# One kernel of a vision tower: thirteen in place of ten gate-up products on GpSimd, and the last two maxima taken apart

## The reference

```python
def _act_fake_quant(x, clip_factor):
    scale = jax.nn.sigmoid(clip_factor) * jnp.max(jnp.abs(x)) / QMAX
    return jnp.clip(_ste_round(x / scale), -QMAX - 1.0, QMAX) * scale
...
xq = _act_fake_quant(x, clip_x[0])
gate = jnp.einsum('bsh,ih->bsi', xq, _weight_fake_quant(w_gate))
up = jnp.einsum('bsh,ih->bsi', xq, _weight_fake_quant(w_up))
h = _act_fake_quant(jax.nn.silu(gate) * up, clip_down[0])
return jnp.einsum('bsi,hi->bsh', h, _weight_fake_quant(w_down))
```

## Time and profile before

| | us |
|---|---|
| median of 3 runs | 151.08 (150.08 to 154.04) |
| the profiled execution | 151.07 |
| its span | 149.1 |
| busy in the span: PE, DVE, ACT, POOL | 119.8, 124.0, 81.4, 36.3 |
| gate-up stage, first matmul to the maximum over the columns | 98.8 to 125.8 |

### The profile page before, as it was taken

One profiled execution on the slowest core, in us unless ns is written; L12 is line 12 of the kernel. 1 busy time (PEld: TensorE's weight loads), 2 busy tenths in 40 slices (PEclk: granted clock), 3 DMA queues, 4 the chain that ended last, 5 costly groups with the idle time before them and its releaser, 6 DMA issues.

```text
span 149.1 us, 1974 instructions
## 1 busy us (share of the span) xinstructions
PE 119.8 (80%) x668; PEld 77.5 (52%) x668; DVE 124.0 (83%) x249; ACT 81.4 (55%) x153; POOL 36.3 (24%) x60
## 2 busy tenths in 40 slices
PE   0759979984978936999999987669999998798710
PEld 0749958972443614854587564235545333564400
DVE  0799998989899849923999798877989898999991
ACT  4004116231694677229961399966999980894000
POOL 6668991000000000000000000003556660005710
PEclk9999999996599998799999999987999999999975
DMA  3999500000000000000000000000000000001276
GB/s 97 388 421 420 228 4 2 0 0 0 0 0 0 7 0 0 0 0 0 0 0 4 0 0 0 0 0 4 0 4 0 0 0 0 4 0 70 85 226 181
DMA packets 2897, 8.01 MB, mean 54 GB/s; under 512 B 453, under 2 KB 709, under 8 KB 2760
## 3 DMA queue, kind: packets, MB, share of 16 engines
q1 hardware_dynamic: 2600, 7.37, 13.5%
q10 hardware_dynamic: 288, 0.52, 0.9%
HBM read 5.79 MB, written 2.10 MB: 53 GB/s over the span
## 4 chain that ended last, share of the span: by engine, by line
PE 35%; DVE 29%; ACT 22%; issue 7%; DMA 3%; POOL 1%; DVEq 0%; ACTq 0%; POOLq 0%
PE bank L557 8%; ACT early L787 7%; PE bank L473 6%; PE bank L413 5%; PE bank L541 4%; DVE middle L1226 4%; PE bank L573 4%; PE bank L443 4%; DVE state_mem L1233 4%; DVE stats L1005 4%; PE bank L617 3%; DVE amax L1199 3%; DVE raw L1258 3%; ACT wqT L771 3%; ACT raw L892 3%
## 5 line engine op out<-in xcount | busy, mean ns | idle before, releaser
L400 POOL TENSOR_TENSOR early<-raw,state_mem 128x512 f32<-128x512 f32 x10 | 12.7, 1272 | 86.9 <-ACT raw L892 86.9
L617 PE MATMUL bank<-state_mem,wqT 128*128 128x512 bf16 x80 | 19.7, 398 | 1.0 <-ACT state_mem L873 0.8
L787 ACT ACTIVATE early<-h,nmr,rstd 128x256 f32<-128x256 f32 x29 | 14.9, 589 | 5.0 <-DVE nmr L1013 5.0
L885 ACT ACTIVATE state_mem<-bank,gscale 128x512 f32<-128x512 f32 x22 | 15.1, 748 | 2.6 <-PE bank L617 2.6
L557 PE MATMUL bank<-mixer_w,early 128*128 128x256 f32 x64 | 15.9, 405 | 0.0
L418 PE MATMUL bank<-restart,ident 128*128 128x512 bf16 x50 | 13.9, 430 | 1.5 <-DVE stats L1005 1.5
L630 PE MATMUL bank<-wqT,middle 128*128 128x256 bf16 (+1 forms) x96 | 12.8, 274 | 2.4 <-DVE middle L1226 2.4
L557 PEld LDWEIGHTS bank<-mixer_w,early 128*128 128x128 f32 x64 | 12.8, 206 | 2.9 <-issue 1.1
L1199 DVE TENSOR_REDUCE amax<-early 128x1 f32<-128x1024 f32 x11 | 13.2, 1212 | 0.5 <-POOL early L400 0.5
L617 PEld LDWEIGHTS bank<-state_mem,wqT 128*128 128x128 bf16 x80 | 7.7, 101 | 10.9 <-issue 1.7
L733 ACT ACTIVATE early<-bank 128x512 f32<-128x512 f32 x8 | 4.7, 598 | 15.6 <-PE bank L413 15.6
(11 more groups left out here) (158 smaller groups left out, 235.7 us busy)
## 6 DMA issues: line engine op xcount, KB each, us to landing
out<-early SPq DMA_DIRECT2D x7, 256.0 KB, 2.7
early<-in_x SPq DMA_DIRECT2D x1, 1024.0 KB, 9.1
wT<-in_dot_weights SPq DMA_DIRECT2D x1, 784.0 KB, 7.0
raw<-in_gate_rows SPq DMA_DIRECT2D x1, 768.0 KB, 9.1
raw<-in_up_rows SPq DMA_DIRECT2D x1, 768.0 KB, 10.5
raw<-in_down_rows SPq DMA_DIRECT2D x1, 768.0 KB, 11.9
early<-in_x ACTq DMA_DIRECT2D x2, 256.0 KB, 4.8
early<-in_x SPq DMA_DIRECT2D x2, 256.0 KB, 4.6
```

The lines of the kernel that those rows point to most:

```text
L400: nc.gpsimd.tensor_tensor(act[:, u, :], up_s[:, m % UPS, :], silu[:, u % SIL, :], ALU.mult).then_inc(pool_act_ready, 1)
L617: last = nc.tensor.matmul(dst[:, :], w, xqT[:, k, c, :], start=(c == 0), stop=(c == CH - 1))
L787: nc.scalar.activation(xn[:, half, r, :], h[:, half, r, :], ACT.Identity, bias=nmr[:, norm, half, r:r + 1], scale=rstd[:, norm, half, r:r ...
L885: nc.scalar.activation(silu[:, u % SIL, :], bank[2 * (u % 3)][:, :], ACT.Silu, scale=gscale[:, 0, t:t + 1]).then_inc(silu_ready, 1)
```

## The change

GpSimd makes the products of all units up to 19 whose number leaves 0 or 1 when divided by 3, unit 0 excepted: 1, 3, 4, 6, 7, 9, 10, 12, 13, 15, 16, 18, 19. VectorE keeps 0, 2, 5, 8, 11, 14, 17, 20, 21. There is one more buffer for the silus and one more for the copies; the copies lie at the end of `raw`, over the last rounded unit, which is written only after the products are all done. The maxima of units 20 and 21 are taken apart, that of 20 ahead of the product of 21, that of 21 last, and `amax` has 12 columns in place of 11. The lines behind the first edits are shifted by one.

```diff
-        SIL, UPS = 5, 2
+        SIL, UPS = 6, 3
...
-        amax = sb("amax", [P, NU // 2])
+        amax = sb("amax", [P, NU // 2 + 1])
...
+        raw.at = raw.floats - UPS * BLK
         up_s = raw.take([P, UPS, BLK])
...
-        POOL_UNITS = range(1, NU - 2, 2)
+        POOL_UNITS = [u for u in range(NU - 2) if u % 3 != 2 and u > 0]
...
-            def pair_maximum(m):
-
-                dve.wait_ge(act_ready, dve_units(2 * m + 2))
-                if pool_units(2 * m + 2):
-                    dve.wait_ge(pool_act_ready, pool_units(2 * m + 2))
-                nc.vector.tensor_reduce(amax[:, m:m + 1], act[:, 2 * m:2 * m + 2, :].rearrange("p a t -> p (a t)"),
+            def unit_maximum(m, first, end):
+
+                dve.wait_ge(act_ready, dve_units(end))
+                if pool_units(end):
+                    dve.wait_ge(pool_act_ready, pool_units(end))
+                nc.vector.tensor_reduce(amax[:, m:m + 1], act[:, first:end, :].rearrange("p a t -> p (a t)"),
                                         AX.X, ALU.max, apply_absolute_value=True).then_inc(amax_ready, 1)
...
                 if u % 2 and u >= 3:
-                    pair_maximum(u // 2 - 1)
-            pair_maximum(NU // 2 - 1)
-            dve.wait_ge(amax_ready, NU // 2)
+                    unit_maximum(u // 2 - 1, u - 3, u - 1)
+                if u == NU - 2:
+                    unit_maximum(NU // 2 - 1, u, u + 1)
+            unit_maximum(NU // 2, NU - 1, NU)
+            dve.wait_ge(amax_ready, NU // 2 + 1)
```

## The result

| | before | changed |
|---|---|---|
| median of the runs, us | 151.25 (6 runs, 150.08 to 154.04) | 152.75 (6 runs, 151.34 to 152.88) |
| ratio of the changed to before | | 1.0111, 95% interval 1.0074 to 1.0147 |
| profiled execution, its span, us | 151.07, 149.1 | 152.63, 150.8 |

The kernel became 1.1% slower: the whole interval lies above 1, and inside the 2% that count as no change. The forecast was 152.8 us. The ratio leaves out the one execution before of 154.04 us, which ran in a slower state of the chip; the median of the other five is 151.08 us.

What follows compares the result with a forecast made beforehand. The prediction took ScalarE, without idle time for 17 us of the gate-up stage, as the bound, with VectorE nearly full. Copies +1.71 and tail +0.05 made +1.76 us on 151.07: 152.8 us, range 151.2 to 153.9.

Steps and rivals of the forecast that it cites:

- Three more copies, +1.71 us: Gate-up stage, ScalarE: three units moved to GpSimd each add a copy of 0.57 us, and nothing hides it: +1.71 us.
- The tail, +0.05 us: From the last silu's start to the maximum over the columns: 4.46 us where it was 4.41, so +0.05 us.
- the first term: The three additional copies on ScalarE in the gate-up stage, +1.71 us of the sum.
- What the split does: End of VectorE's queue: splitting the last maxima saves about 0.5 us behind product 21; the wait for GpSimd returns it.
- Three products fewer on VectorE: worth something only where VectorE sets the end: Gate-up stage: three products leave VectorE, minus 1.98 us of its work, useful only where VectorE sets the end.
- GpSimd keeps up at 89%: Gate-up stage: two GpSimd products take 2.54 us per three units, which last 2.85 us on ScalarE.
- TensorE's clock: Behind the gate-up stage, TensorE's idle time could lower its clock and slow the down matmuls: +0.45 us at most.
- The first rival: Gate-up stage: VectorE sets the end and ScalarE's copies cost nothing: 150.5 us, 12 in 100.
- The second rival: Gate-up stage: GpSimd is slowed beside VectorE and becomes the bound: 154.8 us, 6 in 100.

Runs made afterwards that it cites:

- pairs at thirteen units: The changed kernel with its thirteen GpSimd products, but the maxima in pairs to the end as before: whole time 1.0050 of the kernel before.
- the seven units: The kernel before with larger buffers, GpSimd making seven products in place of ten, three copies fewer on ScalarE: whole time 1.0013 of the kernel before.
- the blocks moved in the kernel before: The kernel before with larger buffers, two moves of quantised input blocks taken from ScalarE to VectorE: whole time 0.9966 of the kernel before.

## Why the prediction was right, and where it was not

*Three more copies, +1.71 us.* Right. From unit 3's silu to the last silu it was 18.91 us in place of 17.28, +1.63, at a pace of 0.57 us without a gap. The prediction put the last silu before at 121.41, one pace behind the one at 120.84; it starts at 121.44. Taking the three copies out alone gave 1.30 us back, making all of them cheaper by 0.09 us gave 0.98.

*The tail, +0.05 us.* Near: 4.48 us from the last silu's start to the maximum over the columns, 4.46 predicted, 4.38 before, so +0.10. The 0.08 too much in the first term and the 0.05 too little here partly cancel in the sum; that is luck, of that size. One step was off without harm. Product 20 was to start at 123.37, when its silu is done; it started at 123.58, because the two maxima queued behind product 17 kept VectorE busy until then. The maximum behind it waits for GpSimd in either case, so only the wait became shorter, 0.21 in place of 0.44 us, and the end stayed. GpSimd's own times were met (product 19 from 123.16 to 124.43, 124.37 predicted).

*What the split does.* Only half told. The prediction said that it saves about 0.5 us behind product 21 and that the wait for GpSimd gives this back. Against pairs at thirteen units it is a loss of 0.34 us: the 0.60 us of the additional instruction and the wait together are more than the 0.5 saved. What nearly balanced the tail is that VectorE came 0.29 us less late to product 20 (1.29 us behind the start of its silu before, 1.00 after), a gain that the prediction used in its sum without naming it. In pairs the tail is 4.12 us, 0.26 shorter than before.

*Three products fewer on VectorE: worth something only where VectorE sets the end.* Right, by the seven units and by the blocks moved in the kernel before.

*GpSimd keeps up at 89%.* Right: 1.27 us each, in pairs, and no gap on ScalarE for a buffer. VectorE's idle time ahead of its products was to be 0.9 us and is 0.76 to 0.85 for products 5 to 17. Behind the stage everything moved by one amount, as said: the maximum over the columns and the first down matmul both by 1.81 us (125.82 to 127.63, 127.99 to 129.80).

*TensorE's clock.* The fall, given 3 in 10 and up to +0.45 us, did not come in the profile above. Its idle time ahead of the transpose was 1.23 us, not 1.8, for its warming matmuls began at 122.99, not about 122.4. In the second profile of the same kernel it did come (a stretch as in the earlier trace rows, and a row of TensorE's timeline):

```profile
130.10:133.40 3.30, 3.30 (x17) 2.09 (x15) 3.26 (x14) 3.30 (x7) 0.00 (x0) 0.50 0.02 5
...
129.86 14.25 PE L631 MATMUL bank<-wqT,middle 64*128 64x256 bf16 x96 [0.98 <-DVE middle L1229]
```

For 3.3 us TensorE worked at half its clock, 1.2 GHz, and yet the 96 down matmuls last 14.25 us from first to last, as in the profile without the fall (129.80 to 144.05). The lost time found room in TensorE's waits for rounded values: in the profile without the fall these show as 0.21 and 1.20 us, in this one as none. From the maximum over the columns to the end of the span it is 23.2 us in both. Nor is the fall tied to the 1.23 us: the kernel with the split alone has one as well, from 129.4 to 132.7 us in its second profile, behind only 0.85 us of idle time.

*The first rival* (VectorE sets the end, ScalarE's copies cost nothing) is refuted by the kernel without three copies and the one with cheaper ones. What spoke for it, the unbroken VectorE, was real: it was the second wall, its product 20 0.7 us behind ScalarE's last silu. *The second rival* (GpSimd slowed by VectorE's accesses) never showed: the thirteen products took 1.270 to 1.282 us each.

## What to carry to other kernels

Moving work to an idle engine is priced by what feeds it: here the 1.27 us on GpSimd cost no more than a wait of 0.21 us at the split maximum, and the 0.57 us copy that gets the operand there landed on the one engine without a gap. Where two engines are both full, a shift from one to the other moves the end by the receiving side's price once it stands first; look for work that neither needs to do, or that is cheaper on the other side (the block moves, 0.9 us on ScalarE and 0.6 on VectorE), before shifting again. When a last step is split to shorten the tail, place the first part where its inputs are already done, or it brings its own wait.

## What the runs showed of the hardware

Behind an ACTIVATE of 128x512 from the bank with a column of scales the next one starts 0.57 us later, behind one without the column 0.48 us. In an unbroken row of them the recorded time of one grows while the pace stays: 0.69 us at 104.24, 0.93 us at 122.01 in the changed kernel. With ten units and the blocks on VectorE, where ScalarE waits now and then, no silu is recorded above 0.71 us. Who reads such durations as cost would put the copies at half as much again. And the granted clock fell at different places in two executions of one and the same kernel, the changed one: between 57.6 and 64.1 us and not again before 145 us in the first profile, from 99.3 to 102.6 and from 130.1 to 133.4 us in the second. Whole times of one kernel spread over 1 us where the stretch repeats to 0.03 us.
